# A transformer layer on one core: one written order per engine in the mixing stage, the feed-forward's norm on ScalarE, late score units one at a time, and a new order of the prologue

## What is computed

```python
qkv = ln(x) @ w_qkv.T + b_qkv            # 16 heads of 16, queries and keys rotated (rope)
attn = softmax(causal(q @ k.T / 4)) @ v
x = x + ln(attn @ w_out.T + b_out)
hidden = silu(ln(x) @ W1.T) * (ln(x) @ W3.T)     # 1024 wide
x = x + ln(fwht(hidden) @ W2.T)          # Walsh-Hadamard transform along the 1024
```

## Time and profile before

| | |
|---|---|
| median of three runs | 500.68 us (498.67 to 501.37) |
| profiled execution | 497.78 us, span 496.1 us, mean granted clock 0.938 |
| TensorE busy | 405.0 us (82%) |
| VectorE busy | 281.2 us (57%) |
| ScalarE busy | 210.9 us (43%) |
| GpSimd busy | 162.1 us (33%) |
| DMA | 36.95 MB |

### The profile page before, as it was taken

The page is one execution under the profiler, slowest core; times in us unless marked ns, Lnnn a source line. Parts: engine busy times, 40 slices in busy tenths (PEclk is TensorE's granted clock), DMA queues, the critical chain, the costliest instruction groups (busy, mean ns, idle before and its releaser), DMA issues.

```text
span 496.1 us, 7892 instructions
## 1 busy us (share of the span) xinstructions
PE 405.0 (82%) x2884; PEld 338.2 (68%) x2884; DVE 281.2 (57%) x936; ACT 210.9 (43%) x314; POOL 162.1 (33%) x284
## 2 busy tenths in 40 slices
PE   1679677999599997988599988987799979858992
PEld 1569645558489985557499975566699965448991
DVE  7554583625937776536856776267576754273114
ACT  4445234753323337843423347813332367423221
POOL 4136002533512226514422235614132245321232
PEclk9999865999969999999889999999799999997998
DMA  6549900000397000200695001102880002000001
GB/s 230 215 136 247 212 1 1 2 2 0 127 255 171 1 1 1 85 1 1 179 245 130 1 1 42 44 1 72 219 201 21 1 1 85 1 1 1 1 1 42
DMA packets 35463, 36.95 MB, mean 74 GB/s; under 512 B 2016, under 2 KB 34528, under 8 KB 35424
## 3 DMA queue, kind: packets, MB, share of 16 engines
q1 hardware_dynamic: 35424, 36.45, 26.6%
HBM read 21.76 MB, written 14.68 MB: 73 GB/s over the span
## 4 chain that ended last, share of the span: by engine, by line
PE 58%; DVE 13%; DMA 9%; issue 7%; ACT 6%; SPq 3%; POOL 2%; DVEq 0%; POOLq 0%; ACTq 0%
PE ps L266 30%; PE ps L448 8%; PE ps L464 7%; PE ps L436 5%; DMA qk_scratch<-qk_s 4%; DMA q_t<-qk_scratch 4%; ACT probs L656 4%; DVE masked_scores L923 2%; SPq L293 2%; DMA raw_bias<-in_b_out 2%; PE ps L498 2%; DVE xy L985 1%; POOL hid_s L803 1%; PE ps L405 1%; DVE stats_h L870 1%
## 5 line engine op out<-in xcount | busy, mean ns | idle before, releaser
L923 DVE CUSTOM_DVE_ANT_0 masked_scores<-ps,mask_row 128x128 bf16<-128x128 f32 (+3 forms) x256 | 114.4, 488 | 61.6 <-PE ps L436 61.1
L266 PE MATMUL ps<-xt,w_s 128*128 128x256 f32 x768 | 111.7, 294 | 0.0
L266 PEld LDWEIGHTS ps<-xt,w_s 128*128 128x128 f32 x768 | 106.2, 202 | 0.5
L803 POOL TENSOR_TENSOR hid_s<-gate,hid_s 128x512 fp32r<-128x512 f32 x32 | 41.2, 1287 | 135.9 <-ACT hid_s L668 135.9
L656 ACT ACTIVATE probs<-ps 128x1280 f32<-128x1280 f32 x64 | 76.4, 1242 | 9.5 <-PE ps L448 8.9
L436 PE MATMUL ps<-k_t,q_t 96*128 96x128 f32 (+3 forms) x256 | 71.7, 356 | 9.8 <-DMA q_t<-qk_scratch 5.6
L448 PEld LDWEIGHTS ps<-q_t,k_t 128*128 128x128 f32 x256 | 44.9, 198 | 32.2 <-ACT probs L656 14.7
L266 PE MATMUL ps<-w_s,hid_s 128*128 128x256 f32 x384 | 55.5, 284 | 7.0 <-POOL hid_s L803 7.0
L448 PE MATMUL ps<-q_t,k_t 128*128 128x512 f32 (+3 forms) x256 | 55.7, 345 | 5.6 <-ACT probs L656 4.0
L266 PEld LDWEIGHTS ps<-w_s,hid_s 128*128 128x128 f32 x384 | 51.6, 190 | 9.3 <-POOL hid_s L803 8.7
L436 PEld LDWEIGHTS ps<-k_t,q_t 96*128 96x128 f32 x256 | 43.0, 198 | 18.6 <-DVE maxima L923 10.9
(11 more groups left out here) (99 smaller groups left out, 485.3 us busy)
## 6 DMA issues: line engine op xcount, KB each, us to landing
qk_scratch<-qk_s SPq DMA_DIRECT2D x32, 256.0 KB, 5.6
k_t<-qk_scratch SPq DMA_DIRECT2D x16, 384.0 KB, 5.5
q_t<-qk_scratch SPq DMA_DIRECT2D x8, 768.0 KB, 8.8
qk_scratch<-qk_s SPq DMA_DIRECT2D x8, 512.0 KB, 5.5
xa<-in_x SPq DMA_DIRECT2D x4, 512.0 KB, 9.6
xy<-in_x SPq DMA_DIRECT2D x4, 512.0 KB, 3.5
out<-xy SPq DMA_DIRECT2D x8, 256.0 KB, 2.3
o_t<-in_w SPq DMA_DIRECT2D x1, 1024.0 KB, 10.0
```

The lines of the kernel that those rows point to most:

```text
L266: ins = eng.matmul(o, lhs(i), rhs(j), start=first and n == 0, stop=last and n == 2, skip_group_check=skip)
L803: pool.tensor_tensor(hid_s[:, a % 2, 1, :], gate[:, a % 2, :], hid_s[:, a % 2, 0, :].bitcast(F32), ALU.subtract).then_inc(S["hid_l"], 1)
L923: ins = dve.tensor_tensor_reduce(masked_scores[:, SCORE_NO[n] % 2, i * keys:(i + 1) * keys], ps[:, banks[n], i * keys:(i + 1) * keys], mas ...
```

## The change

Every engine gets a list of its own for each mixing stage. The values' products are a letter apart (b), as is the table load (S). The norm of the feed-forward goes from VectorE to ScalarE, as an activation with scale and bias, for which GpSimd turns the sign of the shift. Two products of the second hidden block (u4, u5) are taken into the list. The rope has a second sine buffer, rot_s_odd, for odd tiles. Late units stand singly from behind head 2 on, with one pair behind head 3, and `UNITS_AFTER` is another. Value products wait for all maxima but one.

In the prologue the transform of W2 is split: three rounds of additions and subtractions across the blocks on GpSimd (`butterflies`), then one product per block and part with the Hadamard matrix, at unit 33. ScalarE then copies the result to words and to its high part, and VectorE takes the low parts of W2, W3 and W1 during the attention of batch 0. The low part of w_qkv is split between VectorE and GpSimd, the bias is split into that of queries, keys and values and that of the output, the second send waits for the first fetch in batch 0, x is loaded first, and TensorE begins with 14 products on zeros. For batch b+1 the statistics of x stand ahead of the late units of batch 0. What is left out below are the semaphores' names, waits that follow from the new orders (banks shared by letters) and the letters' dispatch.

```diff
-H_BANK = [5, 3, 5, 3]
+H_BANK = [6, 5, 4, 5]
...
-TAIL_AFTER = {4: (0, 2), 5: (2, 4), 6: (4, 6), 7: (6, 7)}
+TAIL_AFTER = {2: (0, 1), 3: (1, 3), 4: (3, 4), 5: (4, 5), 6: (5, 6), 7: (6, 7)}
...
+MIX = {
+    "PE": """q0 o0 o1 n0 n1 o2 o3 y0 b0 n2 y1 n3 y2 q1 r0 y3 b1 q2 b2 r1 q3 r2 b3 r3 H0 H1 u0 H2 u1 H3
+        u4 u2 u3 u5""".split(),
+    "ACT": """n0 q0 n1 n2 n3 b0 q1 S b1 r0 q2 r1 q3 b2 r2 N0 b3 r3 N1 H0 N2 H1 N3 H2 H3 u3""".split(),
+    "DVE": """o0 d0 o1 d1 l0 o2 o3 d2 d3 s0 l1 c0 l2 s1 v0 r0 l3 s2 s3 c1 t0 r1 R0 v1 R1 R2 R3 t1 c2 w0
+        r2 c3 r3 t2 w1 L0 L1 L2 t3 L3""".split(),
+    "POOL": """e0 e1 v0 v1 e2 w0 e3 w1""".split(),
+}
+FIRST_MIX = {
+    "PE": """q0 q1 r0 q2 q3 r1 b0 r2 b1 b2 b3 r3""".split(),
+    "ACT": """q0 q1 q2 r0 q3 r1 b0 b1 b2 r2 r3 b3""".split(),
+    "DVE": """c0 r0 c1 r1 t0 c2 c3 r2 t1 r3 t2 t3""".split(),
+    "POOL": """e0 e1 e2 e3""".split(),
+}
+MIX_LAST = {
+    "PE": """o0 o1 n0 n1 o2 y0 n2 o3 y1 n3 y2 y3 H0 H1 u0 H2 u1 u4 H3 u2 u3 u5""".split(),
+    "ACT": """n0 n1 n2 n3 N0 S N1 N2 N3 H0 H1 H2 H3 u3""".split(),
+    "DVE": """o0 d0 o1 d1 l0 o2 d2 l1 s0 o3 l2 d3 l3 s1 s2 v0 s3 R0 R1 v1 w0 R2 R3 w1 L0 L1 L2 L3""".split(),
+    "POOL": """v0 v1 w0 w1""".split(),
+}
...
-UNITS_AFTER = [(0, 0, 0), (3, 2, 0), (2, 3, 0), (4, 1, 0), (4, 2, 0), (4, 3, 0), (4, 3, 0), (4, 1, 0), (0, 0, 1)]
+UNITS_AFTER = [(0, 0, 0), (4, 2, 0), (1, 1, 0), (5, 1, 0), (7, 2, 0), (2, 1, 0), (5, 2, 0), (3, 2, 0), (0, 0, 3)]
...
+AHEAD = [(1, 0), (1, 1)]
-FIRST_SELECTOR = [None, 0, 2, 9]
-FIRST_TRANSFORM = [-1, -1, -1, -1, -1, 4, 8, 13]
-FIRST_W2_PARTS = [14, 19]
+FIRST_SELECTOR = {2: 0, 3: 2}
+BUTTERFLIES_BEFORE = [0, 4, 13]
+FIRST_W2_PARTS = {"split": 18, "transform": 33, "words": 36, "high": 38}
...
+        rot_s_odd = place("rot_s_odd", [P, 512], word=12176)[:, :]
+        mixed_w2 = place("mixed_w2", [P, HCH * DIM], word=6656)[:, :]
...
                     fetch_q(0)
+                    if b == 0:
+                        sp.wait_ge(S["qk_in"], 48)
                     send(1)
...
             def qkv(b, t):
+                pe.wait_ge(S["xt_l"], b * TILES + t + 1)
...
+                if b == 0 and t == 0:
+                    pe.wait_ge(S["sixty_made"], 1)
+                    pe.wait_ge(S["bias_s"], 1)
+                    pe.wait_ge(S["bias_l"], 1)
...
+            def values_product(b, t):
...
             def values(b, g, kt):
-                        pe.wait_ge(S["maxed"], (b + 1) * N_SCORES)
+                        pe.wait_ge(S["maxed"], (b + 1) * N_SCORES - 1)
...
             def out_product(b, t):
+                if t == 2:
+                    pe.wait_ge(S["normed"], b * TILES + TILES)
...
             def turn_h(b, t):
-                if t >= 2:
-                    pe.wait_ge(S["xt2_l"], b * TILES + t - 1)
+                if t == 1:
+                    pe.wait_ge(S["on_l"], b * TILES + 3)
+                if t == 3:
+                    pe.wait_ge(S["xt2_l"], b * TILES + 2)
...
                     elif m[0] == "u":
-                        up(b, 0, t)
+                        up(b, t // 4, t % 4)
...
-                    if kind == "up":
+                    if kind == "up" and (n, i) not in AHEAD:
                         up(b, n, i)
...
+            def transform():
+                pe.wait_ge(S["had_made"], 1)
+                pe.wait_ge(S["w2_l"], 2)
+                for c in range(HCH):
+                    for part in range(2):
+                        ins = pe.matmul(ps[:, c // 2, (c % 2) * DIM:(c % 2) * DIM + DIM], had_s[:, :],
+                                        w2_s[:, part, c, :], start=(c % 2 == 0 and part == 0),
+                                        stop=(c % 2 == 1 and part == 1), skip_group_check=True)
                 ins.then_inc(S["transformed"], 1)
+            pe.wait_ge(S["zeroed"], 2)
+            for n in range(14):
+                pe.matmul(bank(7), k_t[0:QK_ROWS, 0, 0:P], k_t[0:QK_ROWS, 1, :], start=True, stop=True, skip_group_check=True)
...
+                    elif m[0] == "N":
+                        act.wait_ge(S["ln_h%d" % (t // 2)], 2 * b + 2)
+                        act.activation(y[:, t, :], xr[:, t, :], ACT.Identity, scale=rstd["h"][:, t:t + 1],
+                                       bias=shift["h"][:, t:t + 1]).then_inc(S["norm_h"], 1)
+                    elif m == "S":
                         act.activation(spare[:, :], minus_half[:, 0:1], ACT.Silu)
...
+                if which[0] == "h":
+                    pool.wait_ge(S["ln_" + which], 2 * b + 1)
+                    pool.tensor_scalar(s, s, -1.0, None, ALU.mult).then_inc(S["ln_" + which], 1)
...
+            def butterflies(n):
+                src, dst = (raw_w2, mixed_w2) if n % 2 == 0 else (mixed_w2, raw_w2)
...
+                a, o = (w.rearrange("p (u e n) -> p u e n", e=2, n=DIM << n) for w in (src, dst))
+                pool.tensor_tensor(o[:, :, 0, :], a[:, :, 0, :], a[:, :, 1, :], ALU.add)
+                pool.tensor_tensor(o[:, :, 1, :], a[:, :, 0, :], a[:, :, 1, :], ALU.subtract).then_inc(S["w2_turned"], 1)
...
-                    elif m[0] == "N":
-                        dve.wait_ge(S["ln_h%d" % (t // 2)], b + 1)
-                        dve.tensor_scalar(y[:, t, :], xr[:, t, :], rstd["h"][:, t:t + 1], shift["h"][:, t:t + 1],
-                                          ALU.mult, ALU.subtract).then_inc(S["norm_h"], 1)
...
             def iteration(b, order, steps):
+                if order is MIX:
+                    layer_x(b + 1)
                 if b == 0:
+                    split(w2_s, raw_w2, "transformed_h", 1, "transformed_l")
                     for n in TAIL_UNITS:
                         score_unit(b, n, FIRST_UNIT_BANKS)
+                    split(w3_s, raw_w3, "split_h", 4, "w3_l")
+                    dve.wait_ge(S["transformed_l"], 1)
                 copy_o(b, 0)
                 if order is MIX:
                     norm_x(b + 1)
+                if b == 0:
+                    split(w1_s, raw_w1, "split_h", 3, "w1_l")
...
```

218 lines of the change are left out of this document (116 added, 102 removed).

## The result

The changed kernel takes 493.79 us (median of 4 runs, 493.44 to 494.55) beside 500.34 for the kernel before in the same job: the ratio is 0.9881 [0.9858, 0.9904]. It is faster, but by 1.2% where 3.3% were forecast; the time lies at the edge of the stated range (471 to 494). The profiled run took 493.44 us, its span 491.7 (before 496.1).

The account below looks back on a forecast made before the run. No engine bounds the whole; TensorE's waits cost twice, as idle time and at 1.2 GHz. Terms -7.3 -3.1 -5.4 -2.1 +1.1 = -16.8 from 497.78 give 481.0 us, 483.9 against the median; range 471 to 494.

Parts of the forecast that it names:

- the late units: Attention: score units placed singly from behind head 2 save 0.9 us in batches 1 to 3, 0.4 in batch 0; sum 3.1.
- the feed-forward: Three units ahead of the last down products save half the 1.49 us wait: 0.7 us a batch, 2.1 for three.
- the walk through the four lists up to u0: Mixing stage: following each engine's queue from the last value product puts the first feed-forward product 27.9 us later, 1.8 earlier.
- no extra table loads: ScalarE's norm needs no table load of its own; with loads around every norm the sum would be 10 us worse.
- From V+27.9 on TensorE has work, as it had from 29.7: 1.8 us less per batch: Mixing stage: feed-forward products begin 27.9 us after the last value product, not 29.7, saving 5.4 us in three batches.
- step (b): Prologue: query and key products first, value products later; the late half lands at 54 to 56, not 59.23, gaining 4.5 us.
- held by the send: Rival: a second send only 2 us earlier, or slow additions, leaves the prologue 2 us, not 7.3: 489; chance 0.1.
- Last batch: Mixing without another batch's work: a table load falls into the chain, 1.1 us more, bounds 0 and 2.5.
- only the prologue pays: Rival: mixing waits and 1.2 GHz eat the mixing gain, the norm_z wait the late units' gain: 493.5; chance 0.19.
- Slower: Rival: GpSimd's list delays the mixing and TensorE runs at 1.2 GHz; at 5 us a batch more, 504; chance 0.05.
- The lists pay in full: Rival: half the mixing's idle and low-clock time goes, 5.5 us a batch rather than 1.8: 473; chance 0.2.
- By my walk VectorE ends its last low part when it did before: Mixing stage, argument against full payment: last low part done 30.8 us after the last value product, before at 30.9.

Follow-up runs that it names:

- a7: Changed kernel with the old order of score units over the feed-forward: 496.59 us, ratio 0.9939 to the kernel before.
- a8: Changed kernel with TensorE's waits in the mixing filled by products nobody reads, all lists and waits unchanged: 485.14 us, ratio 0.9695 to the kernel before.
- after: The changed kernel itself, as seen in its profiled run: 493.44 us, span 491.7.
- a3: Changed kernel without the second send's wait for the first fetch in batch 0: 490.38 us, ratio 0.9839 to the kernel before.
- a11: Changed kernel; in the last batch the table load precedes the first norm and the first two tiles' turns precede the other two norms: 492.56 us, ratio 0.9873.
- a2: Changed kernel with the last batch's table load ahead of the first norm on ScalarE: 493.59 us, ratio 0.9902 to the kernel before.
- a15: a14 plus a11's last-batch list, a9's and a3's prologue, and 8 fillers before the prologue's last turn: 477.23 us, ratio 0.9564 to the kernel before.
- a6: Changed kernel with VectorE's and GpSimd's mixing lists reordered so no rope pair stands behind a root of the norm: 486.08 us, ratio 0.9734.
- a14: a10 with the first score units moved behind the second block of up products: 482.41 us, ratio 0.9670 to the kernel before.
- a10: Changed kernel with a6's lists and a8's fillers together, the fillers placed anew: 486.31 us, ratio 0.9742 to the kernel before.
- a12: a10 with the second send of queries and keys held in every batch till the first half is fetched: 485.43 us, ratio 0.9751.
- a13: a10 with the second send waiting for the low parts of the first two normed tiles after batch 0: 485.47 us, ratio 0.9712.
- a9: Changed kernel with the prologue's value products in TensorE's gaps, one before the first turn: 492.99 us, ratio 0.9878 to the kernel before.

## Why the prediction was off in size

- **Right in kind and size:** the late units (forecast 3.1, measured 3.6, 2.55 by taking them back alone), the wait for norm_z (0.4; 0.43), the feed-forward (2.1; 3.2 by stages, of which the units' order is 2.5 by a7), the walk through the four lists up to u0 (R0 at V+14.7; 14.9. Waits 1.9 and 3.8; 1.96 and 3.35. u0 at V+27.9; 28.4), the score stretch of the prologue (waits about as at 63.30, 2.98; 3.23), and no extra table loads (one of Silu and one of Exp a batch), so ScalarE's norm runs beside Silu and Exp without a load of its own. The Trainium skill's "ScalarE: Activation LUTs" ("Table sets: the hidden batching unit") says that identity appears in every set, and the trace agrees: 4 loads at L755 and 4 at L768, and one at the start, as many as before.
- **Mixing, the step "From V+27.9 on TensorE has work, as it had from 29.7: 1.8 us less per batch".** It failed, and gave nothing (+0.8 in three batches) where 5.4 were forecast. u0 came 3.4 us earlier in the three batches together (1.2, 0.9 and 1.3), but two things were not counted. Before, the turns of the normed tiles 2 and 3 stood ahead of u0; now they are behind it and take 0.28 us each from start to start (137.37 to 137.65, 139.07 to 139.35), so 1.7 of the 3.4 are a moved boundary. And the walk priced TensorE's work at one speed: it had the wait before r2 (3.8, measured 3.35) and took it for idle time alone, but the clock stays at the lower level from there for 13.7 us in each batch, where before it was for 10.2, 6.8 and 6.8. With the two turns taken off, the stretch from u0 to the first unit is 2.5 us longer in the three batches for it, more than what was left. a8 shows that it is the clock: the first unit comes 2.4 to 2.6 us earlier in each batch with all lists unchanged. At the full clock the walk itself is right: in a8 u0 stands at V+27.97 (27.9 forecast, 28.4 in after) and VectorE's last low part ends at V+31.0 (30.8 forecast, 33.1 in after). The first paragraph of the prediction says that TensorE's waits cost twice; the sum charged them once.
- **Prologue, step (b).** The first send landed at 31.7 (31.0 forecast, though its own 25.7 and the 6.0 of the earlier trace rows make 31.7), the half at 41.2 (39 to 40.8), the second send took 7.3 instead of 6.0 and the fetch 9.8 (9.7): 58.3 where 54 to 56 stood. By the working's own numbers 40.8, 6.0 and 9.7 already make 56.5, so the forecast gain of 4.5, a late half at 54.7, was the best end of its terms. The wait added before the second send was treated as harmless, and by a3 it costs 2.6 us or more: the second send is ready to go at 35. Of the 5.1 us that the prologue fell short by, 3.7 are the late half (58.3, not 54.6). Of the rest, 0.7 lie between its landing and VectorE's first maxima (59.07), which the sum put at nothing, and 0.5 are ScalarE's copy for the high part of W2, which stands ahead of the last maxima there, done by VectorE at 76.2:

```profile
74.94 1.91 ACT L812 ACTIVATE w_s<-o_t 128x2048 fp32r<-128x2048 f32 x1
```

  This is the rival "held by the send", which gave the prologue 2 us (2.2 measured).
- **Last batch.** +3.9, where +1.1 with a bound of 2.5 was given. After its first turn u0 came 1.3 us later, not 0.5, u2 at 22.9, not 20.7, and the first silu 3.7 late, not 1.1. By a11 the place of the table load and the norms of tiles 2 and 3 ahead of H0 on ScalarE are together 1.9 us at u0 and 1.4 at the end; the walk had blamed the load, which alone a2 shows to be worth 0.4 at u0 and 0.3 at the end. By a8, 1.5 are the clock. a15, which has both cures, is 2.8 shorter and so 1.1 above the kernel before. The waits of 0.93 and 1.27 us, which arise because u0, u1 and u4 run before their followers are ready, are new beside 0.55 before; how much of the rest they are was not tried.
- **The rivals.** The time fell on that of "only the prologue pays" (493.5), and its mechanism was right for the mixing; but the late units did pay, and the prologue did not, so that the number agrees is luck. "Slower" had named what happened, r2's wait making TensorE run u0 to u5 at 1.2 GHz, but it asked for 3.8 us a batch where the mixing lost 0.25. "The lists pay in full", 5.5 us a batch, was not reached by any order tried: from V to the next attention, feed-forward included, a6 takes 3.3 us less than the kernel before and a14, with fillers, 4.0. "By my walk VectorE ends its last low part when it did before" (V+30.9) did not hold at the clock that TensorE had: V+33.1, as above.

## What to carry to other kernels

When a forecast walks through engine queues, price every row behind a wait of TensorE at the clock that rows behind such waits show, and compare by a landmark that has the same work in front of it in both kernels; a stage that ends earlier with less in it has won nothing. Where engines have lists of their own, put an operation for which the long chain waits (here the rope's pair and sum) ahead of one that nobody needs yet (here the root and its statistics). After each gain, look at what lands next: 2 us less of mixing a batch was more than lost in one batch of three, until the first units stood behind the transfer that they read.

## What was not expected of the hardware

- Useless products pay: fillers in waits of 0.75 to 4.9 us took 8.4 us off the span, with the granted clock in the records from 0.890 to 0.946. Of the waits left in the filled kernels, those of 1.51 to 1.68 us before the last turn (a8) had no lower clock behind them, and those of 1.95, 2.22 and 2.33 us for the first half (a10, a12 and a13, batch 1) had 10.2 us of it.
- GpSimd's and VectorE's operations on SBUF hold each other up. In the first 50 us a 128x128 cast on VectorE took 2.26 us beside an addition on GpSimd (VectorE's row, then GpSimd's), where a cast of the same form at 37.38 took 0.22. The four norms of x took 2.89: the one at 9.73 took 1.91 beside GpSimd's 1.85 us for the weights (9.64), the others 0.40 to 0.41 each:

```profile
40.40 2.26 DVE L1164 CAST had_s<-had 128x128 fp32r<-128x128 f32 x1
...
40.05 2.53 POOL L920 TENSOR_TENSOR mixed_w<-o_t 128x1024 f32<-128x1024 f32 x1
...
9.40 2.89 DVE L1024 TENSOR_SCALAR xa<-xa,rstd_x,shift_x 128x256 f32<-128x256 f32 x4 [1.41 <-POOL shift_x L842]
```

  Beside the maxima, which read PSUM, the same additions took 2.34 and 2.35 us. The prediction read the 1.61 us of the rope pair at 133.82 as beside VectorE operations with two SBUF inputs; VectorE's row there is the norm, with one SBUF tensor, and of its three the last took 0.81 us where the others took 0.40.
- ScalarE needs 0.59 us for 256 columns from SBUF with a scale and a bias per partition, and 0.38 for a copy of 256 columns from PSUM: half of the duration for 512 columns (0.32) was too low a bound, and the 0.59 lies above the upper bound of 0.49 too.
- A fetch issued 1.3 us earlier (a9) landed no earlier. And in batch 1 the first half took 17.0 us from the start of its send with the second send beside it (a10) and 17.3 without (a12): the fetch alone was 1.2 us shorter, its send 1.5 longer.
